# Later queries of batch 1 and later Wo loads at the start of a gated attention and expert kernel

## Chip, cores and metric

One Trainium2 chip, one of its cores, one launch. The metric is the device time of the whole kernel in microseconds (us). Of the core's engines, PE (TensorE) multiplies and transposes, DVE (VectorE), ACT (ScalarE) and POOL (GpSimd) work element by element, and SP (SyncE) issues nearly all DMAs.

## What is computed

```python
def _attend(q, k, v):                      # 32 heads of 16, 8 key heads, T = 256
    scores = einsum('bhqd,bhkd->bhqk', q, k) / sqrt(D) + alibi bias
    scores = where(mask, scores, -inf)     # causal, window 64, two sources side by side
    return einsum('bhqk,bhkd->bhqd', softmax(scores), v)

q = heads(concat([ssm_states, hidden_states]) @ Wq, 32)
k, v = heads(hidden_states @ Wk, 8), heads(hidden_states @ Wv, 8)
ssm_k, ssm_v = heads(ssm_states @ Wsk, 8), heads(ssm_states @ Wsv, 8)
x = x + tanh(g_xattn) * (_attend(q, [ssm_k, k], [ssm_v, v]) @ Wo)      # of layernorm(x), ctx_2048
x = x + tanh(g_ffn) * ffn(layernorm(x))    # router over 128 experts, top 4, 8 shared bases, shared part
```

There are 8 batches of 256 tokens of width 512, in float32.

## The kernel before

Every matrix product is made in three passes over operands split into a high and a low part (`PASSES`), so that a projection of 512 or 1024 rows is a run of 12 or 24 matmuls of 128x256. Each engine has a stream of its own, written out by hand, and the streams meet at semaphores alone.

The attention runs in **slots**: slot n makes the scores of one unit of 64 queries and four heads (`scores(n)`, PE L1917, two matmuls), and DVE takes their maxima (`maxima(n)`, L1448). A batch is 32 slots, a head group g is four. Scores of slot n wait until the maxima of slot n-2 are done, since there are two banks. `scores_turned` (L1944) follows 18 slots later, ACT makes the exponentials (L1099), and `times_v` (L1958) multiplies by the values for two groups at a time. In the gaps of each slot PE makes the projections of the next batch: tables (`EARLY_Q`, `Q_PROJ`, `K_PROJ`, `V_PROJ`) say in which slots. Queries come in four parts r = 0 to 3 of 24 matmuls each. Ahead of slot 0 stand the projections of batch 0, the keys of batch 1, and all 24 matmuls of its first query part (`queries(1, 0, ...)`); the second part lies in slots 0 to 7, three matmuls in each (`PIECES`), the third in slots 9 to 11 and the fourth in 12 to 14. ACT and DVE take each part out of PSUM (`q_high` L1080, `q_low` L1425).

The scores read **stacked** operands, `KS` (k_stack) and `QS` (q_stack), whose rows DATA to FINE hold the three passes of 16 dimensions. They are filled for each head group by DMAs from SP. For the keys it goes through DRAM: `keep_k(b)` (L580) writes three copies of 256 KB, and `stack_k(b, g)` (L596) reads 192 KB back. For the queries there are two ways. In batches 2 to 6 `keep_q(b)` (L586) writes three copies of 512 KB, and `stack_q` (L619) reads 192 KB back for each group. In batches 0, 1 and 7 (`straight(b)`) each group is copied directly within SBUF by three DMAs of 64 KB (`stack_q_direct`, L603). Before slot 0, SP issues in this order: the loads of weights and rows, `keep_k(0)`, the four loads of Wo (L562), for g = 0 to 7 the keys and queries of batch 0, and `keep_k(1)`. In the slots it then issues the stacks of batch 1, group g, in slot 22 + 4g; each waits until PE has done with the same group of batch 0.

The queries of batch 1 have a buffer of their own (`Q1`, second_qT), since those of batch 0 are still being copied. `oT` takes the transposed outputs (`o_high` on ACT, L1110; `o_low` on POOL, L822), first in slot 32. Wo is staged in four pieces in `wo_stage`; ACT and POOL split it in slots 12 to 15 (`SPLIT_WO`), and it is first used in slot 56.

## Time and profile before

| | |
|---|---|
| median of 3 runs | 889.38 us (888.36 to 889.59) |
| the profiled execution | 888.36 us, its span 886.3 us |
| PE busy | 870.2 us, 98% of the span |
| DVE, POOL, ACT busy | 61%, 58%, 45% |
| PE waited for others in the first 75 us | 5.4 us in 14 places |
| first scores, slot 0 | at 34.85 us |
| DMA traffic | 110.17 MB, mean 124 GB/s |

Times in a trace are counted from the start of the span. A matmul's row shows its start and how long it took; since matmuls are pipelined, the distance between two starts, not the duration, is what one costs. What stands in square brackets is how long the engine sat idle before it and what released it. Two states of the PE clock occur, 2.4 GHz (shown as 1.00) and 1.2 GHz (0.50).

### The profile page before, as it was taken

The page shows a single profiled execution, that of the slowest core. Times are in us where ns is not written, and L with a number is a line of the kernel's source. Part 1 is how long each engine was busy: PE and PEld are TensorE (multiplying, and loading weights), DVE is VectorE, ACT ScalarE, POOL GpSimd, SP SyncE. Part 2 cuts the span into 40 slices and gives each one's busy share as a digit, 9 for nine tenths or more (in the row PEclk, how much of TensorE's full clock was granted, in tenths as well). Part 3 has the DMA queues.
Part 4 walks back from the last instruction along what each step waited for, and adds up shares of the span by engine and source line. Part 5 has one row for each costly group of instructions (what it writes and reads, how often), then busy time and mean ns, then how long its engine had stood idle before and what let it go on. Part 6 is the DMA issues. An engine that isn't in the chain of part 4 may idle for free.

```text
span 886.3 us, 17380 instructions
## 1 busy us (share of the span) xinstructions
PE 870.2 (98%) x6662; PEld 757.5 (85%) x6662; DVE 537.9 (61%) x983; ACT 400.5 (45%) x810; POOL 510.1 (58%) x526
## 2 busy tenths in 40 slices
PE   8999999999999999999999999999999999999998
PEld 7889999999999997778888867888888888888886
DVE  6675666666667666533246748466565565565567
ACT  5655555454545455463134243444444444444431
POOL 3861434435353513161679984456788888788741
PEclk9999999999999999899999999999999999999999
DMA  8677576767767655760101244402202021121046
GB/s 269 171 153 183 148 202 185 193 184 188 203 176 203 164 145 131 206 215 13 36 25 48 84 142 158 166 25 71 72 25 96 25 71 35 61 72 48 1 139 241
DMA packets 77947, 110.17 MB, mean 124 GB/s; under 512 B 7329, under 2 KB 49058, under 8 KB 76834
## 3 DMA queue, kind: packets, MB, share of 16 engines
q1 hardware_dynamic: 75656, 108.04, 42.8%
q10 hardware_dynamic: 2210, 1.03, 0.5%
q8 instruction: 53, 0.87, 0.4%
q14 instruction: 28, 0.23, 0.1%
HBM read 71.76 MB, written 32.05 MB: 117 GB/s over the span
## 4 chain that ended last, share of the span: by engine, by line
PE 91%; DVE 4%; issue 1%; POOL 1%; DMA 1%; ACT 1%; SPq 0%; DVEq 0%; POOLq 0%
PE ps_scores L2158 20%; PE ps_proj L1807 13%; PE ps_scoresT L2158 10%; PE ps_scoresT L1944 6%; PE ps_scores L1796 6%; PE ps_o L1958 6%; PE ps_proj L1796 5%; PE ps_scores L1917 5%; PE ps_scoresT L1796 5%; PE ps_proj L2158 5%; PE ps_proj L1865 5%; DMA xn_rows<-in_x 1%; PE ps_o_max L1976 1%; DVE neg_max L1448 1%; PE ps_o_max L1845 1%
## 5 line engine op out<-in xcount | busy, mean ns | idle before, releaser
L1099 ACT ACTIVATE probsT<-ps_scoresT 128x512 f32<-128x512 f32 (+1 forms) x256 | 138.0, 544 | 153.1 <-PE ps_scoresT L1944 148.8
L1448 DVE TENSOR_REDUCE neg_max<-ps_scores 128x2 f32<-128x384 f32 (+1 forms) x256 | 131.2, 516 | 111.1 <-PE ps_scores L1917 110.4
L1315 ACT ACTIVATE part_sums<-ps_scores 128x512 f32<-128x512 f32 x96 | 57.4, 598 | 134.6 <-PE ps_scores L2158 130.2
L1944 PE MATMUL ps_scoresT<-q_stack,k_stack 116*128 116x256 f32 x448 | 106.5, 310 | 1.7 <-ACT probsT L1099 1.6
L1917 PE MATMUL ps_scores<-k_stack,q_stack 114*128 114x192 f32 (+1 forms) x512 | 96.2, 270 | 4.7 <-DVE neg_max L1448 3.8
L816 POOL TENSOR_TENSOR o_normal<-o_blocks,inv_sums 128x256 f32<-128x256 f32 x32 | 19.9, 622 | 130.6 <-DVE inv_sums L1469 130.6
L1917 PEld LDWEIGHTS ps_scores<-k_stack,q_stack 114*128 114x128 f32 x512 | 82.3, 191 | 11.6 <-DVE neg_max L1448 3.8
L962 POOL TENSOR_TENSOR w_expert_lo<-w_sums,w_expert_hi 128x256 fp32r<-128x256 f32 x64 | 63.8, 1007 | 45.5 <-ACT w_expert_hi L1238 45.5
L974 POOL TENSOR_TENSOR big<-big,basis 128x512 f32<-128x512 f32 x56 | 77.5, 1402 | 14.9 <-DVE basis L1746 14.9
L1944 PEld LDWEIGHTS ps_scoresT<-q_stack,k_stack 116*128 116x128 f32 x448 | 70.2, 191 | 6.3 <-ACT probsT L1099 2.8
L1737 DVE TENSOR_TENSOR basis<-part_sums,silu_gate 128x512 f32<-128x512 f32 x32 | 24.2, 755 | 67.3 <-ACT silu_gate L1323 67.3
L1807 PE MATMUL ps_proj<-actT_hi,wq_hi 128*128 128x256 f32 x224 | 63.6, 284 | 0.4 <-DVE second_qT_lo L1425 0.4
L1807 PE MATMUL ps_proj<-actT_lo,wq_hi 128*128 128x256 f32 x224 | 63.3, 283 | 0.0
L1807 PE MATMUL ps_proj<-actT_hi,wq_lo 128*128 128x256 f32 x224 | 63.3, 283 | 0.0
L822 POOL TENSOR_TENSOR oT_lo<-oT_raw,oT_hi 128x256 fp32r<-128x256 f32 x32 | 23.6, 737 | 67.3 <-ACT oT_hi L1110 67.3
L1746 DVE TENSOR_TENSOR basis<-basis,big 128x512 f32<-128x512 f32 x56 | 56.8, 1015 | 1.0
L1958 PE MATMUL ps_o<-probsT,v_ones 128*32 128x128 f32 (+1 forms) x2048 | 56.9, 264 | 0.0
L1958 PEld LDWEIGHTS ps_o<-probsT,v_ones 128*32 128x32 f32 x2048 | 51.5, 111 | 3.6 <-issue 0.3
L1716 DVE TENSOR_TENSOR part_sums<-part_sums,ps_scoresT 128x512 f32<-128x512 f32 x32 | 22.0, 687 | 53.6 <-ACT part_sums L1315 53.6
L962 POOL TENSOR_TENSOR w_expert_lo<-w_raw,w_expert_hi 128x256 fp32r<-128x256 f32 x48 | 45.8, 968 | 11.2 <-ACT w_expert_hi L1238 11.1
L2158 PE MATMUL ps_scores<-xnT_hi,w_expert_lo 128*128 128x512 f32 x128 | 49.8, 389 | 0.0
L2158 PE MATMUL ps_scores<-xnT_hi,w_expert_hi 128*128 128x512 f32 x128 | 49.8, 389 | 0.0
(302 smaller groups left out, 2491.8 us busy)
## 6 DMA issues: line engine op xcount, KB each, us to landing
k_stack<-k_kept SPq DMA_DIRECT2D x64, 192.0 KB, 4.3
big<-coeff_rows SPq DMA_DIRECT2D x8, 1024.0 KB, 4.7
q_stack<-q_kept SPq DMA_DIRECT2D x40, 192.0 KB, 4.2
q_kept<-qT_hi SPq DMA_DIRECT2D x10, 512.0 KB
x_rows<-in_x SPq DMA_DIRECT2D x9, 512.0 KB, 6.5
k_kept<-kT_hi SPq DMA_DIRECT2D x16, 256.0 KB
x_kept<-x_rows SPq DMA_DIRECT2D x16, 256.0 KB, 3.0
w_raw<-in_L_ffn_w_gate SPq DMA_DIRECT2D x16, 256.0 KB, 2.9
```

Of the source, the lines that this page charges most:

```text
L962: pool.tensor_tensor(WS[n % 2]["lo"][:, w, :], w_source(n, w), WS[n % 2]["hi"][:, w, :].bitcast(F32), ALU.subtract).then_inc(e_lo, 1)
L974: pool.tensor_tensor(dst, dst, BS[:, j, :], ALU.add).then_inc(acc_done, 1)
L1099: act.activation(PT[:, g % 2, 2 * j:2 * j + blocks].rearrange("p h f r w -> p (h f r w)"), ST[:, n % 2, 0:blocks].rearrange("p h n -> p (h ...
L1315: act.activation(TP[:, u % 2, j, :], src[:, u % 2, :], ACT.Copy).then_inc(taken, 1)
L1448: dve.tensor_reduce(NM[:, g // 2 % 2, g % 2, 2 * i:2 * i + 2], SA[:, n % 2, :, 0:keys], AX.X, ALU.max, negate=True).then_inc(max_done, 1)
L1746: dve.tensor_tensor(dst, BS[:, j, :], cB[:, k % 2, group_columns(t)], ALU.mult).then_inc(basis_done, 1)
L1796: ins = pe.matmul(out, stat(s, c), mov(m, c), start=c == cs[0] and j == 0, stop=c == cs[-1] and j == PARTS - 1)
L1807: ins = pe.matmul(out, stat(s, c), mov(m, c), start=i == 0, stop=i == len(steps) - 1, skip_group_check=True)
L1917: ins = pe.matmul(SA[:, n % 2, f, 0:2 * (near.stop - near.start)], QS[0:TOP, g, i, f].rearrange("p r w -> p (r w)"), keys[:, near, :].rear ...
L1944: ins = pe.matmul(ST[:, n % 2, v, :], KS[0:ROWS, g, j + v, 1 - v].rearrange("p w s -> p (w s)"), QS[0:ROWS, g, j + v].rearrange("p f r w - ...
L1958: ins = pe.matmul(POB[32 * r:32 * r + 2 * D, n % 2, j * W:j * W + cols_j], VA[:, j, n % HK, :], PT[:, n % 2, 2 * j:2 * j + cols_j // W, :, ...
L2158: ins = pe.matmul(bank[:, u % 2, :], WS[n % 2][s][:, w, c * P:(c + 1) * P], operand(MEETS[w], m, c, g), start=first and c == 0 and j == 0, ...
```

## The change

It does five things.

1. **Queries of batch 1.** Only the first 12 matmuls of part 0 stay ahead of slot 0. The other 12 go into slots 1, 3, 5 and 7, three in each (`EARLY_PIECES`). Parts 1, 2 and 3 lie in slots 9 to 11, 11 to 13 and 13 to 15.
2. **Wo.** Its four loads leave the head of SP's queue. Two are issued in slot 24 and two in slot 28 (`LOAD_WO`), into X1 and a smaller `wo_stage`; they are split in slots 34 to 37 (`SPLIT_WO`). The load of X1's rows in slot 42 waits for the split of the second.
3. **Stacks of batch 1.** Groups 0 and 1 alone are still copied directly (`DIRECT`). For groups 2 to 7 `keep_q(1)` is issued behind `keep_k(1)`, ahead of the slots, and each group is then one read of 192 KB.
4. **Buffers.** `Q1` moves to where `oT` lies. So ACT's first `o_high`, in slot 32, no longer waits for the split of Wo but for `keep_q(1)` to have landed and for the direct copies of groups 0 and 1; POOL's first `x1_normalise` loses its wait for the copies.
5. **Tables.** Rows and context of batches 3 and on are loaded three slots earlier (`LOAD_ROWS`), the gates six slots earlier, tanh four.

```diff
-LOAD_ROWS, STATS = -61, (-51, -50)
+LOAD_ROWS, STATS = -64, (-51, -50)
-EARLY_Q = ((-1, -1, 7), (-1, -1, 8), (9, 10, 11), (12, 13, 14))
-PIECES = 8
+EARLY_Q = ((-1, -1, 7), (9, 10, 11), (11, 12, 13), (13, 14, 15))
+DIRECT = 2
+EARLY_PIECES = {1: 4, 3: 5, 5: 6, 7: 7}
-SPLIT_WO = 12
+LOAD_WO, SPLIT_WO = (24, 28), 34
-TANH, LOAD_GATES = 54, 44
+TANH, LOAD_GATES = 50, 38
...
-    wo_stage = at("wo_stage", 184 * KIB, [P, HC, HID])
+    wo_stage = at("wo_stage", 216 * KIB, [P, 2, HID])
-    Q1 = {h: at(f"second_qT_{h}", (216 - n * 8) * KIB, [P, NB, 2, G, HQ], F32R) for n, h in enumerate(("hi", "lo"))}
+    Q1 = {h: at(f"second_qT_{h}", (184 + n * 4) * KIB, [P, NB, 2, G, HQ], F32R) for n, h in enumerate(("hi", "lo"))}
...
-    def straight(b):
-        return b in (1, B - 1)
+    def straight(b, g):
+        return b == B - 1 or (b == 1 and g < DIRECT)
...
-            sp.wait_ge(q_kept, 16 * PARTS * (b - 1))
+            sp.wait_ge(q_kept, 16 * PARTS * b)
...
-        for n in range(FIRST_O, len(halves)):
-            weight(n)
         for g in range(HK):
             stack_k(0, g)
             stack_q_first(g)
...
         keep_k(1)
+        keep_q(1)
...
+            if n in LOAD_WO:
+                for m in range(2):
+                    weight(FIRST_O + 2 * LOAD_WO.index(n) + m)
...
             elif c == 0:
-                wait_split(act, len(halves) - 1)
+                act.wait_ge(q_kept, 16 * PARTS)
+                for g in range(DIRECT):
+                    act.wait_ge(q_in[g], q_loads(1, g))
...
         keys_values("k", 1, 1)
-        queries(1, 0, 1, 2)
...
-            if n < PIECES:
-                queries(1, 1, n, PIECES)
+            if n in EARLY_PIECES:
+                queries(1, 0, EARLY_PIECES[n], 8)
```

The order of SP's instructions behind the last stack of batch 0, first before and then after the change. k_kept and q_kept are the copies in DRAM.

```order
50 L580 DMA k_kept<-kT_hi 8x16x512 x2
51 L580 DMA k_kept<-kT_lo 8x16x512
52 L596 DMA k_stack<-k_kept 48x4x256
53 L603 DMA q_stack<-second_qT_hi 16x1024
54 L603 DMA q_stack<-second_qT_lo 16x1024
55 L603 DMA q_stack<-second_qT_hi 16x1024
56 L596 DMA k_stack<-k_kept 48x4x256
```

```order
49 L583 DMA k_kept<-kT_hi 8x16x512 x2
50 L583 DMA k_kept<-kT_lo 8x16x512
51 L589 DMA q_kept<-second_qT_hi 8x16x1024
52 L589 DMA q_kept<-second_qT_lo 8x16x1024
53 L589 DMA q_kept<-second_qT_hi 8x16x1024
54 L599 DMA k_stack<-k_kept 48x4x256
55 L606 DMA q_stack<-second_qT_hi 16x1024
56 L606 DMA q_stack<-second_qT_lo 16x1024
57 L606 DMA q_stack<-second_qT_hi 16x1024
58 L565 DMA x_rows<-in_L_xattn_Wo 128x512 x2
59 L599 DMA k_stack<-k_kept 48x4x256
```

Three writes of 512 KB now stand ahead of group 0 of batch 1, and two loads of Wo between its groups 0 and 1. On PE, slots 1 and 2 before the change, and slots 0 to 3 after it:

```order
206 L1917 MATMUL ps_scores<-k_stack,q_stack 128x192 x2
207 L1807 MATMUL ps_proj<-actT_hi,wq_hi 128x256
208 L1807 MATMUL ps_proj<-actT_hi,wq_lo 128x256
209 L1807 MATMUL ps_proj<-actT_lo,wq_hi 128x256
210 L1917 MATMUL ps_scores<-k_stack,q_stack 128x192 x2
211 L1807 MATMUL ps_proj<-actT_hi,wq_hi 128x256
```

```order
191 L1921 MATMUL ps_scores<-k_stack,q_stack 128x128 [waits stack_in0]
192 L1921 MATMUL ps_scores<-k_stack,q_stack 128x128
193 L1921 MATMUL ps_scores<-k_stack,q_stack 128x192 x2
194 L1811 MATMUL ps_proj<-actT_hi,wq_hi 128x256
195 L1811 MATMUL ps_proj<-actT_hi,wq_lo 128x256
196 L1811 MATMUL ps_proj<-actT_lo,wq_hi 128x256
197 L1921 MATMUL ps_scores<-k_stack,q_stack 128x192 [waits max_done]
198 L1921 MATMUL ps_scores<-k_stack,q_stack 128x192
199 L1921 MATMUL ps_scores<-k_stack,q_stack 128x192 [waits max_done]
200 L1921 MATMUL ps_scores<-k_stack,q_stack 128x192
```

Before, three matmuls of a projection stand behind each pair of scores; after, behind every second pair.

## Rows read from the trace of the kernel before

**Rows 1.** Page, parts 1 (busy us, share) and 5 (busy us, mean ns, idle before).
```profile
PE 870.2 (98%) x6662; PEld 757.5 (85%) x6662; DVE 537.9 (61%) x983; ACT 400.5 (45%) x810; POOL 510.1 (58%) x526
...
L1448 DVE TENSOR_REDUCE neg_max<-ps_scores 128x2 f32<-128x384 f32 (+1 forms) x256 | 131.2, 516 | 111.1 <-PE ps_scores L1917 110.4
```

**Rows 2.** Waits of PE, whole span: engine, line, waited for, us in total, times, longest.
```profile
PE ps_scores L1917 <- DVE neg_max L1448: 3.8, 10, 1.1
```

**Rows 3.** Timeline of PE, slots 0 to 17: start, us taken, engine, line, operation.
```profile
34.03 0.28 PE L1807 MATMUL ps_proj<-actT_hi,wq_lo 128*128 128x256 f32 x1
34.15 0.28 PE L1807 MATMUL ps_proj<-actT_lo,wq_hi 128*128 128x256 f32 x1
34.85 0.44 PE L1917 MATMUL ps_scores<-k_stack,q_stack 114*128 114x128 f32 x2 [0.41 <-DMA q_stack<-qT_hi]
...
37.88 0.44 PE L1917 MATMUL ps_scores<-k_stack,q_stack 114*128 114x128 f32 x2 [0.44 <-DMA q_stack<-qT_hi]
...
41.84 0.39 PE L1807 MATMUL ps_proj<-actT_hi,wq_hi 128*128 128x256 f32 x1 [0.38 <-DVE second_qT_lo L1425]
...
49.82 0.47 PE L1917 MATMUL ps_scores<-k_stack,q_stack 114*128 114x192 f32 x2 [0.46 <-DVE neg_max L1448]
```

**Rows 4.** Timeline of DVE around slot 0.
```profile
27.50 0.78 DVE L1425 TENSOR_TENSOR qT_lo<-ps_scoresT,qT_hi 128x256 fp32r<-128x256 f32 x2
...
33.71 0.69 DVE L1418 TENSOR_TENSOR kT_lo<-ps_proj,kT_hi 128x512 fp32r<-128x512 f32 x1 [2.47 <-ACT kT_hi L1071]
35.32 0.42 DVE L1448 TENSOR_REDUCE neg_max<-ps_scores 128x2 f32<-128x256 f32 x1 [0.92 <-PE ps_scores L1917]
```

**Rows 5.** Timeline of SP's DMA issues: start, us that the issue took.
```profile
20.91 1.37 SPq L580 DMA_DIRECT2D k_kept<-kT_hi  x2
...
29.68 0.65 SPq L596 DMA_DIRECT2D k_stack<-k_kept  x1
30.43 0.62 SPq L603 DMA_DIRECT2D q_stack<-qT_hi  x1
...
52.14 1.33 SPq L580 DMA_DIRECT2D k_kept<-kT_hi  x2
...
60.03 0.60 SPq L596 DMA_DIRECT2D k_stack<-k_kept  x1
```

**Rows 6.** Timeline of SP, batch 2: its query writes and the stacks behind them.
```profile
93.37 0.65 SPq L586 DMA_DIRECT2D q_kept<-qT_hi  x1
...
97.65 1.71 SPq L596 DMA_DIRECT2D k_stack<-k_kept  x1
106.34 0.35 SPq L619 DMA_DIRECT2D q_stack<-q_kept  x1
```

**Rows 7.** The k_stack load issued at 97.65: from issue to landing, us.
```profile
DMA to landing us min/median/max: 11.0/11.0/11.0
```

**Rows 8.** Windows: stretch, us, busy of each engine, granted clock, DMA share, GB/s.
```profile
55.00:58.00 3.00, 3.00 (x28) 2.95 (x26) 1.76 (x4) 2.46 (x5) 2.97 (x3) 1.00 0.52 188
101.00:104.00 3.00, 3.00 (x60) 2.69 (x62) 1.71 (x4) 0.67 (x3) 0.00 (x0) 1.00 0.53 203
350.00:352.00 2.00, 1.05 (x8) 0.84 (x8) 1.11 (x4) 0.97 (x3) 2.00 (x3) 1.00 0.84 269
...
354.00:356.00 2.00, 2.00 (x33) 1.74 (x35) 1.16 (x2) 0.61 (x2) 0.00 (x0) 0.50 0.95 255
```

**Rows 9.** Timeline of PE: slot 32, a times_v at 2.4 GHz, one at 1.2 GHz.
```profile
66.50 0.34 PE L1917 MATMUL ps_scores<-k_stack,q_stack 114*128 114x128 f32 x2
...
69.59 1.74 PE L1958 MATMUL ps_o<-probsT,v_ones 128*32 128x128 f32 x64
...
354.61 2.73 PE L1958 MATMUL ps_o<-probsT,v_ones 128*32 128x128 f32 x64
```

**Rows 10.** Timeline of ACT in slots 32 and 33.
```profile
67.66 0.41 ACT L1110 ACTIVATE oT_hi<-oT_raw 128x256 fp32r<-128x256 f32 x1
68.55 0.39 ACT L1099 ACTIVATE probsT<-ps_scoresT 128x256 f32<-128x256 f32 x1 [0.48 <-PE ps_scoresT L1944]
```

More of the change, by code:

```diff
@@ L175, in projections @@
 def projections():
-    order = [("k", 0, 0), ("v", 0, 0)] + [("q", 0, r) for r in range(G)] + [("k", 1, 0), ("q", 1, 0), ("q", 1, 1)]
+    order = [("k", 0, 0), ("v", 0, 0)] + [("q", 0, r) for r in range(G)] + [("k", 1, 0), ("q", 1, 0)]
     for n in range(SLOTS):
@@ L382, in staging @@
         if n >= FIRST_O:
-            return wo_stage[:, n - FIRST_O, :]
+            return (X1, wo_stage)[(n - FIRST_O) // 2][:, (n - FIRST_O) % 2, :]
         return stage[:, n % 8, :]
@@ L438, in queries_of, with q_loads @@
         return Q1 if b == 1 else Q
-    def straight(b):
-        return b in (1, B - 1)
-    def q_loads(b):
-        return 16 * sum(PARTS if straight(i) else 1 for i in range(1, b + 1))
+    def straight(b, g):
+        return b == B - 1 or (b == 1 and g < DIRECT)
+    def q_loads(b, g):
+        return 16 * sum(PARTS if straight(i, g) else 1 for i in range(1, b + 1))
     def wait_rows(eng, g):
@@ L557, in weight @@
                 wait_split(sp, n - 8)
+            if n == FIRST_O:
+                sp.wait_ge(prep_t, 2 * TB)
             src = halves[n][0]
@@ L613, in stack_q @@
             sp.wait_ge(st_mm, (b - 1) * UNITS + NB * (g + 1))
-            if straight(b):
+            if straight(b, g):
                 sp.wait_ge(pj_done, passed("q", b, G - 1))
@@ L675, in _ @@
                 else:
-                    sp.wait_ge(prep_t, 2 * TB)
+                    wait_split(sp, FIRST_O + 1)
                 sp.dma_start(X1[:], x_t[:, b]).then_inc(x1_in, 16)
@@ L692, in _ @@
                 for g in range(HK):
-                    sp.wait_ge(q_in[g], q_loads(B - 1))
+                    sp.wait_ge(q_in[g], q_loads(B - 1, g))
                 router = cols(a["L0_ffn_w_router"], 0)
@@ L834, in x1_normalise @@
                 pool.wait_ge(xT_mm, TB * b)
-            elif t == 0:
-                for g in range(HK):
-                    pool.wait_ge(q_in[g], q_loads(1))
             if 1 <= b <= SPILLED:
@@ L1077, in q_high @@
             elif b >= 3 and r == 0:
-                act.wait_ge(q_kept, 16 * PARTS * (b - 2))
+                act.wait_ge(q_kept, 16 * PARTS * (b - 1))
             act.wait_ge(q_mm, G * b + r + 1)
@@ L1910, in scores @@
                 if b >= 1:
-                    pe.wait_ge(q_in[g], q_loads(b))
+                    pe.wait_ge(q_in[g], q_loads(b, g))
             if n >= 2:
@@ L2069, in _ @@
                     b = queries_due(n, r, part)
-                    if b is not None and (b > 1 or r > 1):
+                    if b is not None and (b, r) != (1, 0):
                         queries(b, r, part)
```

## Prediction

> **What bounds the kernel now.** The page comes first: PE is busy for 98% of the span [rows 1], and the change neither adds nor removes a matmul. So it can only take away or add time in which PE stands still, or time at its lower clock. The waits of PE over the whole span say where it stands [rows 2]: the longest sum, for the maxima, is 3.8 us in ten places. Third, the timeline of PE in slots 0 to 17 shows the waits that this change can reach [rows 3]: 0.41 and 0.44 us for the query copies of groups 0 and 1, 0.38 us for a bank, 0.46 us for a maximum. Each costs more than its idle time: from the start at 34.15 to that at 34.85 are 0.70 us where a matmul costs 0.12. Counted so, they are worth some 3 us, the ceiling of the gain at the front. Then I read the queue of SP, since the change loads it in a new place.
>
> **The front, slots 0 to 17.** One matmul of a projection costs 0.12 us (34.03 to 34.15 [rows 3]). Twelve of them leave the stretch ahead of slot 0, so PE reaches slot 0 at 34.27 - 12 x 0.12 = 32.8 us. Is the first stack there? Its keys were issued at 29.68 us, when the writes of `keep_k(0)` had landed, 8.8 us after their first issue at 20.91 [rows 5]. Wo's 1 MB was loaded beside them. 768 KB at the 188 GB/s of such writes alone [rows 8] take 4.1 us, so without Wo they should be there at about 27.5. The query copies then wait for the low part of the queries, at 27.50 + 0.78 = 28.3 us [rows 4], and go out at 28.4 instead of 30.43 [rows 5]: 2.1 us earlier, and with them all stacks of batch 0, each group four issues behind the last. The first copies, which PE got at 34.85, it now gets at 32.8. That fits.
>
> But DVE is not ready. It takes the low part of batch 1's keys at 33.71, whose matmuls end when they did, and is free at 34.3 instead of starting its first maximum at 35.32 [rows 4]. The gain there is 1.0 us. From then on slots 0 to 7 hold 16 score matmuls and 12 others, about 3.1 us of PE, but eight maxima in a ring with the scores, at 0.516 us each [rows 1]: slot 8 comes at about 38 us, PE stands still for about 2 us on the way, and slots 9 to 15 then hold 72 projection matmuls, 8.6 us, instead of 48. The bank wait of 0.38 us and the wait at 49.82 [rows 3] go, because matmuls now stand where the scores were alone. Carried through, slot 18 starts about 0.8 us earlier. Bounds: 1.9 us earlier, if half of PE's still time in slots 0 to 7 is filled better than I assume; 0.5 us later, if group 2 is late by a slow issue. I take **-0.8 us**.
>
> **The stacks of batch 1.** SP ends with batch 0's stacks at 50.0 instead of 52.1 and issues `keep_k(1)`. Behind it now stand three writes of 512 KB, and in front of slot 32 still the keys and direct copies of group 0. What such a queue does is to be seen in batch 2 [rows 6]: first query write issued at 93.37, all landed at 106.34, 13.0 us later; the key load issued behind them, at 97.65, landed 11.0 us after its issue [rows 7], that is after the writes, not beside them. While queries or keys are written the DMA share is 0.53 and 0.52 and the rate 203 and 188 GB/s [rows 8]: half of the 16 engines work, and a load that needs all 16 waits for that half. For batch 1: keys' writes end 2 us earlier than before, at 57.5 (before 60.03 at the latest [rows 5]); 1.5 MB at 203 GB/s are 7.7 us; the writes end at 65.2. Then come group 0's keys and its three copies, about 2.1 us with their landing. Group 0 is there at 67.3. PE wants it in slot 32, at 66.50 [rows 9] less 0.8, or 65.7. **+1.6 us**. Bounds: 0, if the key writes finish by 54.5 and the queries' follow at once; 3.5, if the query writes also show the 13.0 us of batch 2, counted from the release of the keys' half.
>
> On this the Trainium skill has two rules, both in "DMA: Bandwidth & Descriptors". In "Why a DMA increments its semaphore by 16 and not by 1" a DMA runs on the largest number of engines up to 16 that divides its slowest dimension: these writes are 8x16x1024 (the order shows it), so on 8, and the trace agrees with its share of 0.53. Its "Specifications" give about 27 GiB/s for an engine. As an estimate from that page 8 engines move 232 GB/s, the writes take 6.8 us, and the wait would be 0.7 us instead of 1.6; the trace's 203 GB/s stands against it, and the sum goes by the trace.
>
> **ACT's new wait.** In slot 32 ACT makes the first `o_high`, before at 67.66 [rows 10]. It now waits for the copies of group 1 too, and these stand behind two loads of Wo (512 KB) and group 1's keys: some 3 us behind group 0, at about 70.4. ACT gets to it at 67.3 + 1.2 = 68.5. Queued behind it is the exponential of slot 33, before at 68.55 for 0.39 us, which `times_v` at 69.59 [rows 9, 10] waits for: the slack is 0.65 us. Now `o_high` ends at 70.8 and the exponential at 71.2, while PE could use it at 70.5. **+0.7 us**. Bounds: 0 (the slack covers it, or group 0 is late by so much that group 1 is not later still) and 2.5 us (issues of 1.7 us each, as the one at 97.65 [rows 6], for the four ahead of it).
>
> **The clock.** In the 2 us from 350 the PE was busy for 1.05, and from 354 to 356 the granted clock was 0.50, that is 1.2 instead of 2.4 GHz [rows 8]; a `times_v` then took 2.73 instead of 1.74 us [rows 9]. A stand of 1.6 us in slot 32, with sparse slots (29 to 31) before it and a second wait soon after, is a gap of the same size. I take one such fall, with one slow `times_v`, **+1.0 us**. Bounds: 0, and 1.7 if the whole low stretch is filled with matmuls.
>
> **Edits at nothing.** The split of Wo leaves ACT and POOL in slots 12 to 15, where nobody waited for them, and comes to slots 34 to 37; POOL's `scale_outputs` is about 2 us later there, and DVE's turn of it in slot 37 half a us, one slot ahead of the next scores that could feel it. If that cover is gone it costs 0.5 us. Rows and context three slots earlier, gates and tanh: their users are ten and more slots behind them. Five issues fewer on SP are only worth something where SP is late, which is behind slot 32.
>
> **Sum:** -0.8 + 1.6 + 0.7 + 1.0 = +2.5 us. Against the profiled execution that is 888.36 + 2.5 = 890.9 us; this was the fastest of the three, 1.0 us under the median, so I give it against the median: 889.38 + 2.5 = **891.9 us**.
>
> **Rivals.**
> 1. *The stacks are in time.* If the writes of keys and queries end by 63, group 0 lands before 65.7 and only the front is left: -0.8, 888.6 us. For it: batch 2's slow start may belong to its writes alone, and keys ahead of them may cover it; SP is 2 us earlier. Against it: 11.0 us [rows 7]. It decides when the writes end before 63.5. With the front at its best, -1.9 to -2.5 us, it would be 887.2 us.
> 2. *The waits come, the clock stays.* +1.5 us, 890.9 us. For it: other sparse stretches of the front do not lower the clock.
> 3. *Issues behind a full queue are slow.* The load at 97.65 took 1.71 us to issue [rows 6], the others 0.6. With such issues for all of groups 0 and 1, group 1 lands some 3 us later and ACT's wait counts in full: +2.5 + 3.0 = +5.5 us, 894.9 us.
> 4. *Slots 0 to 7 are too sparse*, and the clock falls there too: +1.0 to +1.7 on any of the others.
>
> **How the numbers follow.** The forecast has 0.36, the first rival 0.24 at 888.6 and 0.10 at 887.2, the second 0.18, the third and fourth together 0.12. What a measurement of this kernel can tell from no change is about 0.2%, 1.8 us: below 887.6 is faster, above 891.2 slower. Slower: the forecast, the third and fourth, and the upper end of the second, 0.53. Faster: the best front and a little of the first, 0.13. The rest, 0.34, within. Range: from 887.6 (1.8 us gained, near the best front) to 895.2 (the third rival and a little more).
>
> **What the profile would show.** Right: PE's first scores at 32.8 and first maximum at 34.3; slot 8 at 38; slot 18 under a us earlier; PE idle for one to three us ahead of slot 32 with a DMA as its releaser; `o_high` idle for a us or more behind q_stack copies; a granted clock of 0.50 somewhere from 66 to 75. Wrong: group 0 of batch 1 landed before PE asked (first rival); DVE not the pace of slots 0 to 7; a stand at another place, such as slots 34 to 38, which would be the split of Wo.

## The result and the profile after

The changed kernel takes 894.24 us (median of 6 runs, 892.6 to 894.64), the kernel before, run beside it, 889.25 us (885.26 to 890.02). The ratio is 1.006, with a 95% interval of 1.0042 to 1.0079: **slower by 0.6%**. The profiled execution took 892.44 us, its span is 890.4 us.

The page of the changed kernel, parts 1 and 5, against [rows 1]:

```profile
PE 872.0 (98%) x6662; PEld 758.9 (85%) x6662; DVE 539.8 (61%) x983; ACT 400.1 (45%) x810; POOL 509.9 (57%) x526
...
L1452 DVE TENSOR_REDUCE neg_max<-ps_scores 128x2 f32<-128x384 f32 (+1 forms) x256 | 130.9, 516 | 110.2 <-PE ps_scores L1921 109.5
```

The instructions are the same in number and PE's share is the same. PE is busy 1.8 us longer with the same work, so part of the loss is a low clock and not idle time. The waits of PE in the first 75 us (engine, line, waited for: us in total, times, longest) name the rest:

```profile
PE ps_o L1962 <- ACT probsT L1101: 1.3, 1, 1.3
PE ps_scores L1921 <- DVE neg_max L1452: 1.2, 3, 0.7
PE ps_scores L1921 <- DMA q_stack<-qT_hi: 1.2, 1, 1.2
...
PE ps_scores L1921 <- issue: 0.7, 1, 0.7
...
PE ps_proj L1869 <- DMA q_stack<-second_qT_hi: 0.2, 1, 0.2
```

To place the loss, I read the same instructions in both timelines of PE: the first scores of slots 0, 20, 28 and 32, and the start of the fourth `times_v`.

| PE starts, us | slot 0 | slot 20 | slot 28 | slot 32 | fourth `times_v` |
|---|---|---|---|---|---|
| before | 34.85 | 52.17 | 61.86 | 66.50 | 91.85 |
| after | 32.40 | 53.67 | 63.34 | 68.79 | 95.76 |
| difference | -2.45 | +1.50 | +1.48 | +2.29 | +3.91 |

Behind that the two run in step: from the fourth `times_v` to the end of the span are 794.4 us before and 794.6 us after. So there are three losses: 3.9 us between slots 0 and 20 (1.4 of it are the 12 matmuls that moved there), 0.8 us in slot 32, and 1.6 us right behind it.

**The front.** Timeline of PE in the changed kernel, slots 0 to 8 (columns as in [rows 3]):

```profile
32.40 0.69 PE L1921 MATMUL ps_scores<-k_stack,q_stack 114*128 114x128 f32 x4
...
34.13 0.93 PE L1921 MATMUL ps_scores<-k_stack,q_stack 114*128 114x192 f32 x4 [0.66 <-DVE neg_max L1452]
...
36.65 0.69 PE L1921 MATMUL ps_scores<-k_stack,q_stack 114*128 114x128 f32 x4 [1.21 <-DMA q_stack<-qT_hi]
...
38.63 0.28 PE L1811 MATMUL ps_proj<-actT_lo,wq_hi 128*128 128x256 f32 x1
38.81 1.14 PE L1921 MATMUL ps_scores<-k_stack,q_stack 114*128 114x128 f32 x4
...
41.24 0.41 PE L1811 MATMUL ps_proj<-actT_hi,wq_hi 128*128 128x256 f32 x1
41.45 0.41 PE L1811 MATMUL ps_proj<-actT_hi,wq_lo 128*128 128x256 f32 x1
```

Windows of the same kernel (columns as in [rows 8]):

```profile
35.00:38.80 3.80, 2.59 (x18) 2.05 (x18) 2.24 (x6) 3.78 (x8) 3.80 (x5) 1.00 0.65 129
38.80:42.20 3.40, 3.40 (x17) 3.35 (x17) 1.96 (x6) 1.32 (x4) 1.11 (x2) 0.50 0.71 141
42.20:45.00 2.80, 2.80 (x25) 2.80 (x25) 1.90 (x4) 0.00 (x0) 0.00 (x0) 0.99 0.85 260
```

PE stood for 0.66 us behind DVE and for 1.21 us behind the query copies of group 1, and was busy for 2.59 of 3.80 us. The copy it stood for is group 1's last. SP issued it in time, but it was long on its way (SP's row, and the landing times of group 1's last two copies, of which the 4.5 us are this one's):

```profile
32.09 0.58 SPq L606 DMA_DIRECT2D q_stack<-qT_hi  x1
...
DMA to landing us min/median/max: 2.9/3.7/4.5
```

Then the granted clock was 0.50, 1.2 GHz, from 38.8 to 42.2 us. In that stretch the distance between two matmuls of a projection is 0.21 us (41.24 to 41.45) instead of 0.12. Low for 3.4 us costs 1.7 us.

**Slot 32 and `o_high`.** SP's issues in the changed kernel (start, us taken):

```profile
52.25 0.75 SPq L589 DMA_DIRECT2D q_kept<-second_qT_hi  x1
...
58.03 0.59 SPq L599 DMA_DIRECT2D k_stack<-k_kept  x1
59.13 0.66 SPq L606 DMA_DIRECT2D q_stack<-second_qT_hi  x1
59.84 1.35 SPq L606 DMA_DIRECT2D q_stack<-second_qT_lo  x1
61.23 2.21 SPq L606 DMA_DIRECT2D q_stack<-second_qT_hi  x1
63.55 1.24 SPq L565 DMA_DIRECT2D x_rows<-in_L_xattn_Wo  x2
```

The key load of 58.03, from issue to landing in us:

```profile
DMA to landing us min/median/max: 9.9/9.9/9.9
```

A window of the same kernel while the writes run, with a DMA share of 0.55:

```profile
54.00:57.00 3.00, 3.00 (x27) 3.00 (x27) 1.72 (x4) 1.72 (x4) 0.71 (x1) 1.00 0.55 207
```

The timeline of PE, slot 32 and the second half of the `times_v` behind it:

```profile
68.79 0.41 PE L1921 MATMUL ps_scores<-k_stack,q_stack 114*128 114x128 f32 x2 [0.66 <-issue]
...
74.26 0.97 PE L1962 MATMUL ps_o<-probsT,v_ones 128*32 128x128 f32 x32 [1.33 <-ACT probsT L1101]
```

And that of ACT, `o_high` and the exponential behind it:

```profile
73.52 0.42 ACT L1114 ACTIVATE oT_hi<-oT_raw 128x256 fp32r<-128x256 f32 x1 [3.40 <-DMA q_stack<-second_qT_hi]
73.84 0.37 ACT L1101 ACTIVATE probsT<-ps_scoresT 128x256 f32<-128x256 f32 x1
```

Group 0's keys land at 58.03 + 9.9 = 67.9 us and its last copy at 68.7; PE starts at 68.79. ACT stands still for 3.40 us for the copies of group 1, and the exponential behind `o_high` holds up the second half of `times_v` by 1.33 us.

### The profile page after: what moved, and what is told of

It reads as the page before. It is cut to its first block, busy times and chain, and to the rows that moved or that the text cites. A ratio compares the mean times of both kernels' runs of the same rounds, so it can differ in the third digit from the quotient of the medians.

```text
span 890.4 us, 17369 instructions
## 1 busy us (share of the span) xinstructions
PE 872.0 (98%) x6662; PEld 758.9 (85%) x6662; DVE 539.8 (61%) x983; ACT 400.1 (45%) x810; POOL 509.9 (57%) x526
## 4 chain that ended last, share of the span: by engine, by line
PE 89%; DVE 3%; DMA 3%; issue 1%; SPq 1%; POOL 1%; ACT 1%; DVEq 0%; POOLq 0%; ACTq 0%
PE ps_scores L2161 20%; PE ps_proj L1811 13%; PE ps_scoresT L2161 10%; PE ps_scoresT L1948 6%; PE ps_scores L1800 6%; PE ps_o L1962 6%; PE ps_proj L1800 5%; PE ps_scores L1921 5%; PE ps_scoresT L1800 5%; PE ps_proj L2161 5%; PE ps_proj L1869 4%; DMA xn_rows<-in_x 1%; DMA q_stack<-second_qT_hi 1%; DVE neg_max L1452 1%; PE ps_o_max L1980 1%
## 5 line engine op out<-in xcount | busy, mean ns | idle before, releaser
L821 POOL TENSOR_TENSOR o_normal<-o_blocks,inv_sums 128x256 f32<-128x256 f32 x32 | 19.9, 621 | 129.7 <-DVE inv_sums L1473 129.7
L1741 DVE TENSOR_TENSOR basis<-part_sums,silu_gate 128x512 f32<-128x512 f32 x32 | 24.2, 755 | 67.3 <-ACT silu_gate L1327 67.3
L1811 PE MATMUL ps_proj<-actT_lo,wq_hi 128*128 128x256 f32 x224 | 63.7, 284 | 0.0
L1962 PE MATMUL ps_o<-probsT,v_ones 128*32 128x128 f32 (+1 forms) x2048 | 57.5, 265 | 1.3 <-ACT probsT L1101 1.3
L1750 DVE TENSOR_TENSOR basis<-basis,big 128x512 f32<-128x512 f32 x56 | 56.8, 1015 | 1.0
```

Source lines behind the costliest of these rows:

```text
L1750: dve.tensor_tensor(dst, BS[:, j, :], cB[:, k % 2, group_columns(t)], ALU.mult).then_inc(basis_done, 1)
L1811: ins = pe.matmul(out, stat(s, c), mov(m, c), start=i == 0, stop=i == len(steps) - 1, skip_group_check=True)
L1962: ins = pe.matmul(POB[32 * r:32 * r + 2 * D, n % 2, j * W:j * W + cols_j], VA[:, j, n % HK, :], PT[:, n % 2, 2 * j:2 * j + cols_j // W, :, ...
```

## The experiments

One table first, all from profiled executions. "Low" is the stretch before 90 us in which the granted clock was 0.50. The last columns are the medians and the ratio to the kernel before, run beside each; medians of different rows come from different sets of runs, so kernels are compared by the ratio. e1 to e5 and e11 have 4 to 6 runs each, the others 12.

| run | slot 0 | slot 20 | slot 32 | fourth `times_v` | low | median | ratio (95%) |
|---|---|---|---|---|---|---|---|
| before | 34.85 | 52.17 | 66.50 | 91.85 | none | | |
| after | 32.40 | 53.67 | 68.79 | 95.76 | 38.8 to 42.2 | 894.24 | 1.0060 (1.0042, 1.0079) |
| e1 | 33.41 | 50.53 | 69.81 | 96.70 | 66.2 to 73.0 | 892.09 | 1.0063 (1.0038, 1.0089) |
| e2 | 34.32 | 56.13 | 70.46 | 95.79 | 35.1 to 45.3 | 892.13 | 1.0062 (1.0039, 1.0085) |
| e3 | 33.14 | 55.29 | 69.62 | 95.88 | none | 891.83 | 1.0060 (1.0035, 1.0085) |
| e4 | 33.80 | 52.94 | 72.57 | 100.84 | 68.7 to 78.9 | 895.38 | 1.0093 (1.0064, 1.0122) |
| e5 | 32.84 | 51.57 | 69.15 | 97.12 | 68.0 to 74.8 | 894.15 | 1.0069 (1.0046, 1.0091) |
| e6 | 32.28 | 52.19 | 66.52 | 91.85 | 36.5 to 39.9 | 887.61 | 0.9987 (0.9971, 1.0004) |
| e7 | 34.04 | 51.18 | 65.49 | 90.82 | none | 887.52 | 0.9982 (0.9968, 0.9995) |
| e8 | 34.37 | 51.91 | 66.25 | 93.14 | none | 887.06 | 0.9991 (0.9976, 1.0007) |
| e9 | 33.87 | 50.99 | 65.29 | 94.27 | 74.7 to 78.1 | 887.37 | 0.9982 (0.9969, 0.9995) |
| e10 | 33.35 | 50.47 | 67.13 | 93.47 | 66.0 to 69.4 | 890.64 | 1.0020 (1.0009, 1.0032) |
| e11 | 33.58 | 52.54 | 66.85 | 104.39 | 76.1 to 86.3 | 897.86 | 1.0105 (1.0085, 1.0125) |
| e12 | 34.44 | 51.56 | 65.87 | 91.20 | none | 886.57 | 0.9979 (0.9964, 0.9994) |

### e1 and e2: each half of the change at the front

e1 is the changed kernel with the query tables of before:

```diff
-EARLY_Q = ((-1, -1, 7), (9, 10, 11), (11, 12, 13), (13, 14, 15))
-EARLY_PIECES = {1: 4, 3: 5, 5: 6, 7: 7}
+EARLY_Q = ((-1, -1, 7), (-1, -1, 8), (9, 10, 11), (12, 13, 14))
+PIECES = 8
```

> The changed kernel with the query tables of before: all 24 matmuls of part 0 of batch 1 ahead of slot 0, part 1 in slots 0 to 7 with three matmuls in each, parts 2 and 3 in slots 9 to 14. Wo late, query writes and new buffers stay. Theory A (the front is too sparse): slot 0 now starts at 34.3 us, slots 0 to 8 run at 0.58 us each, the granted clock stays at 1.00 from 30 to 50 us, slot 18 starts at about 50.0 instead of 51.95 us, and the time falls by 1 to 2 us, if the waits at slots 32 to 34 don't take it back. Rival B (the queue of DMAs alone made the loss, slots 0 to 18 are only shifted work): slot 18 stays near 51.9 us and the time as it is. Rival C (the stacks of batch 1 come at a fixed time): slot 18 is earlier, but PE then waits longer ahead of slot 32 and the exponential of slot 33, so that slot 36 starts when it does in the changed kernel and the time is the same within 0.5 us.

The front is 3.1 us faster than in the changed kernel (slot 20 at 50.53 against 53.67), with no low clock there. But slot 32 starts 1.0 us **later**, and the ratio is the same 1.006. The waits of PE in e1 (columns as above):

```profile
PE ps_scores L1921 <- issue: 4.8, 1, 4.8
```

Two windows of e1, before and in this stand:

```profile
62.00:66.00 4.00, 2.56 (x15) 1.79 (x14) 2.64 (x7) 1.32 (x3) 2.46 (x2) 1.00 0.70 200
66.00:70.00 4.00, 0.18 (x1) 0.22 (x2) 0.00 (x0) 0.00 (x0) 0.00 (x0) 0.52 1.02 233
```

PE comes to slot 32 early, stands for 4.8 us until 69.81 (the profile names no releaser), and the clock falls there, as the prediction had it for this place. Group 0's last copy, issued from 62.92 to 64.81, is what lands last, at 69.7. What the front gains, slot 32 takes.

e2 is the kernel before with the new query tables alone (the opposite of the diff above).

> The kernel before with only the new query tables (12 matmuls of part 0 in slots 1, 3, 5 and 7, parts 1 to 3 in slots 9 to 15); Wo early, all copies of batch 1 direct. Theory A (sparse front): slots 0 to 7 are paced by the maxima and by the stacks, which come as in the kernel before (slot 8 at 40.5 us); slots 9 to 15 carry 24 matmuls more, 2.9 us, so slot 18 starts 1 to 2.5 us later than 50.78, more if the clock falls, and the time is 1 to 3 us above the kernel before. Rival B (front harmless): slot 18 within 0.5 us of 50.78 and the same time.

From slot 0 to slot 20 it takes 21.8 us; before it was 17.3. Of the 4.5 us more the 12 moved matmuls are 1.4. The other 3.1 lie in a stretch with 10.2 us of low clock (half of that, 5.1 us, is the most that it can cost) and 0.49 us of standing in slot 4. A window of e2 just as the low clock begins:

```profile
32.00:35.00 3.00, 1.43 (x13) 1.23 (x12) 0.89 (x2) 2.90 (x6) 3.00 (x5) 1.00 0.64 141
35.00:38.00 3.00, 2.51 (x13) 2.16 (x11) 1.71 (x4) 3.00 (x8) 3.00 (x4) 0.52 0.79 158
```

PE was busy for 1.43 of 3 us and then ran at 1.2 GHz. The timeline of PE in e2, slot 0:

```profile
34.32 0.69 PE L1917 MATMUL ps_scores<-k_stack,q_stack 114*128 114x128 f32 x4 [1.57 <-DMA q_stack<-qT_hi]
```

The new query places alone cost 0.6%, without any query write in the queue: its slot 32 has no wait, and from there to the fourth `times_v` it takes 25.33 us, as the kernel before (25.35). Theory A held against its rival, with a loss of 5.5 us by the ratio where it had 1 to 3. So the late group 0 is not the only way to lose 0.6%. In e2 Wo is still loaded early, group 0 of batch 0 lands only at 34.2 us, and PE, which has 12 matmuls fewer ahead of slot 0, stands there for 1.57 us.

### e3: filling the sparse slots

The changed kernel with three idle matmuls of 128x256 each in slots 0, 2, 4 and 6, whose result nobody reads:

```diff
+            if n in (0, 2, 4, 6):
+                ones = VA[:, 0].rearrange("p g e -> p (g e)")
+                for _ in range(3):
+                    pe.matmul(POB[:, :, :].rearrange("p h n -> p (h n)")[:, 0:T], ones[:, 0:P], ones[:, 0:T], start=True, stop=True)
```

> The changed kernel with three idle matmuls of 128x256 (ones by ones, into a free bank) added in each of slots 0, 2, 4 and 6, where PE stands still for the maxima; 1.4 us of work that nobody reads. Theory A1 (the fall of the clock is what costs at the front): the granted clock stays at 1.00 between 38 and 43 us, slot 12 starts 1 to 1.7 us earlier than 45.27 us, slot 18 at about 50.6. Rival A2 (only the pace of the maxima and the late copies of group 1 cost): the clock stays up but slot 12 starts no earlier, or later by the 1.4 us added. If slot 18 is earlier by 1.5 us, the time falls by 0 to 1.5 us, by how much the stacks of batch 1 let it.

The clock stays high up to 350 us. This one trace doesn't show that the filling did it, since e4, e5 and e11 have the unfilled front of the changed kernel and no fall there either. The mean granted clock of all runs says more: 0.996 to 1.000 in the five runs of e3, 0.992 or 0.994 in the eight of the changed kernel on record. But the time didn't follow. The 12 idle matmuls, 1.4 us, and whatever else is longer take more than the fall did: 22.2 us from slot 0 to slot 20 against 21.3. Rival A2 won. PE then comes to slot 32 at 69.62, when group 0's last copy has landed at 69.5, so nearly without a stand. The fourth `times_v` is where it was (95.88 against 95.76), and so is the ratio.

### e4: Wo out of the way of group 1

```diff
-LOAD_WO, SPLIT_WO = (24, 28), 34
+LOAD_WO, SPLIT_WO = (26, 30), 34
```

> The changed kernel with the loads of Wo issued in slots 26 and 30 instead of 24 and 28, that is behind the stacks of group 1 and group 2 and no longer ahead of them. Theory (ACT's wait for the copies of group 1 is made by what stands ahead of them on SP): the copies of group 1 are issued 1.3 us earlier, o_high starts 1.2 to 2 us earlier than 73.52 us, PE's wait of 1.33 us at times_v of slot 34 goes, the time falls by about 1.3 us. Rival (the copies of group 1 wait for the query writes like those of group 0): o_high at 73 us or later, no change in the time.

Neither the theory nor its rival foresaw the result, 1.0093; its interval overlaps that of the changed kernel, so that it is slower than that isn't shown. `o_high` (at 74.29, not 1.2 to 2 us earlier than 73.52) no longer stands idle, but only because PE is later: group 0 is. Its query writes were issued 1.0 us later (53.25 against 52.25) and took longer, and the last of the direct copies landed at 72.5 instead of 68.7. The timeline of PE in e4, slot 32:

```profile
72.57 0.66 PE L1921 MATMUL ps_scores<-k_stack,q_stack 114*128 114x128 f32 x2 [5.16 <-DMA k_stack<-k_kept]
```

The window in which this stand ends, at 1.2 GHz:

```profile
70.00:74.00 4.00, 1.43 (x7) 1.46 (x8) 0.42 (x1) 0.20 (x1) 0.00 (x0) 0.50 0.99 215
```

That the moved Wo made the writes slower isn't shown: it is issued after group 0. The executions with the same writes differ (below), and 4 runs are few. What is shown is that this order of the loads behind the writes doesn't help.

### e5: only group 0 copied directly

```diff
-DIRECT = 2
+DIRECT = 1
```

> The changed kernel with group 0 of batch 1 alone copied directly; group 1 is one read of q_kept. ACT's first o_high then waits for the q_kept writes and for group 0. Theory (a group's landing is set by the query writes, which landed at 66.9 us, and the wait of o_high for group 1, 3.40 us idle and 1.33 us of it on PE, is a cost of its own): group 0 lands at 68.7 as before, o_high starts by about 70.5 instead of 73.5, the wait of PE for probsT at 74.3 goes, and the whole is 1.3 us shorter, about 892.9. Rival (the time lost at o_high is only the time lost at slot 32 seen a second time): the same as the changed kernel, 894.2.

The part on `o_high` held: it starts without a wait and 2.7 us earlier, and PE's wait for probsT is gone. The timeline of PE in e5, slot 32:

```profile
69.15 0.66 PE L1921 MATMUL ps_scores<-k_stack,q_stack 114*128 114x128 f32 x2 [3.10 <-DMA k_stack<-k_kept]
```

The timeline of ACT in e5, `o_high`:

```profile
70.87 0.41 ACT L1114 ACTIVATE oT_hi<-oT_raw 128x256 fp32r<-128x256 f32 x1
```

The forecast of 1.3 us gained fell: 894.15 us, ratio 1.0069. In this execution the front had no low clock (slot 20 at 51.57), PE came early, stood for 3.10 us, and the clock was low from 68.0 to 74.8 instead. From slot 32 to the fourth `times_v` are 27.97 us, more than the 26.97 of the changed kernel, although the wait on ACT is gone. The median is that of the rival, the trace has the mechanism of the theory. My reading is that the wait is a cost of its own, and that what is saved went to the stand and the fall at slot 32. One trace doesn't prove it; the mean granted clock of its runs, 0.988 to 0.992 against 0.992 and 0.994 in the changed kernel, fits it.

### e6 and e7: writes of 128 rows

In both kernels the three passes of a dimension are laid side by side in DRAM, and in the rows DATA to FINE. A write of keys is then 128 rows of 512 and one of queries 128 rows of 1024, not 8 blocks of 16 rows. Bytes and number of DMAs are the same. e6 is the changed kernel so, e7 the kernel before:

```diff
-    q_kept_d = nc.dram_tensor("q_kept", (2, HK, PARTS, D, 2 * NB * 2 * W), F32).ap()
+    q_kept_d = nc.dram_tensor("q_kept", (2, HK, D, PARTS, 2 * NB * 2 * W), F32).ap()
...
-                sp.dma_start(q_kept_d[b % 2, :, j], queries_of(b)[part][:].rearrange("p i f r w -> p (i f r w)").bitcast(F32)
+                sp.dma_start(q_kept_d[b % 2, :, :, j].rearrange("g d n -> (g d) n"), queries_of(b)[part][:].rearrange("p i f r w -> p (i f r w)").bitcast(F32)
...
-                sp.dma_start(QS[DATA + j * D:DATA + (j + 1) * D, g].rearrange("p i f r w -> p (i f r w)").bitcast(F32),
+                sp.dma_start(QS[DATA + j:FINE:PARTS, g].rearrange("p i f r w -> p (i f r w)").bitcast(F32),
```

> The changed kernel with the layout in DRAM and of the rows DATA to FINE changed from (pass, dimension) to (dimension, pass), so that a write of keys or queries is 128 rows of 512 or 1024 instead of 8 blocks of 16. Theory (the writes run on half of the engines and this sets group 0's landing): the DMA share in the stretch of the query writes rises from 0.55 to over 0.8, they land at about 63 instead of 66.9, group 0 at about 65 instead of 68.7, before PE asks for it in slot 32; issues of 0.6 us instead of 1.3 and 2.2; group 1 lands about 3 us earlier, so o_high costs PE little. 2.2 us gained, about 892. The clock fall at 39 us stays. Rival (the rate of 200 GB/s is that of DRAM or of the queue, not of the number of engines): landing at 67 as before, 894.2.

This is the run that bears most on the main cause. Two windows of e6, while the keys and the queries are written (the second holds group 0's load and copies too):

```profile
50.00:54.00 4.00, 3.80 (x29) 3.34 (x29) 3.26 (x8) 2.12 (x5) 3.24 (x2) 1.00 1.03 326
54.00:58.00 4.00, 4.00 (x36) 3.98 (x35) 2.29 (x5) 3.05 (x6) 0.00 (x0) 1.00 1.01 371
```

SP's issues for group 0 in e6:

```profile
54.31 0.57 SPq L599 DMA_DIRECT2D k_stack<-k_kept  x1
55.38 0.88 SPq L606 DMA_DIRECT2D q_stack<-second_qT_hi  x1
56.31 0.58 SPq L606 DMA_DIRECT2D q_stack<-second_qT_lo  x1
56.93 0.59 SPq L606 DMA_DIRECT2D q_stack<-second_qT_hi  x1
```

The timeline of ACT in e6, `o_high`, with no idle time before it:

```profile
67.68 0.41 ACT L1114 ACTIVATE oT_hi<-oT_raw 128x256 fp32r<-128x256 f32 x1
```

The share nearly doubles, from 0.55 to 1.01, and the rate rises from 207 to 371 GB/s. On this the Trainium skill's rule in "DMA: Bandwidth & Descriptors", section "Why a DMA increments its semaphore by 16 and not by 1", holds: 128 is a multiple of 16, so all 16 engines should work, and the share of 1.01 agrees.

Group 0's copies, 3.6 us at most from issue to landing, are there at 60.4 instead of 68.7, eight us earlier, where I had expected 65. PE doesn't wait in slot 32, `o_high` starts at 67.68 as in [rows 10], and the fourth `times_v` at 91.85, as before the change. The low clock in front is still there (36.5 to 39.9). The new layout gave back all of the 3.9 us that the profile had lost. But only 2.4 of them are the waits of slot 32 (0.8) and behind it (1.6). The other 1.5 were there at slot 20 already (52.19 against 53.67), before the query writes had landed: PE has no wait for query copies in front. The layout also changes the key writes of batch 0 (group 0's keys are issued at 24.07 us instead of 27.46) and the rows that the direct copies fill, and e6 doesn't tell these apart from the luck of one execution: e5, with narrow writes, came to slot 20 earlier still, at 51.57.

The gain is more than the 2.2 us expected: 6.6 us between the medians 894.24 and 887.61, which come from two sets of runs. The mean granted clock rose with it, from 0.992 or 0.994 to between 0.994 and 1.000 in the 12 runs of e6.

e6 and e2 have the same query places. In e6 Wo is late and group 0 of batch 0 in time, and slot 0 starts at 32.28 instead of 34.32. That may be why the new places cost 0.6% in one kernel and nothing that shows in the other; no run separates it.

> The kernel before with the same layout as the run above. Theory: the first key writes (issued at 20.9, last landing about 29.6) end up to 3 us earlier, so that the first group is in its place when PE has ended its projections at 34.3, and DVE with its first maximum at 34.3 to 35 is the next thing late: 0.4 to 0.9 us gained, 888.4 against 889.2. Rival (a load beside them, Wo, takes what they leave, and SP's issues pace the stacks): no change, 889.2. If the ratio is over 1.0, the wide writes cost elsewhere (batches 2 to 6).

e7 is faster than the kernel before by 0.2%, with an interval below 1: the wide writes need no other part of the change. Slot 0 starts at 34.04, `times_v` at 90.82, 1.0 us earlier. No kernel below with parts of the change added to it is faster than e7's 0.9982 by more than the noise.

### e8: the late Wo alone

```diff
-SPLIT_WO = 12
+SPLIT_WO = 28
...
-        for n in range(FIRST_O, len(halves)):
-            weight(n)
         for g in range(HK):
...
         keep_k(1)
+        for n in range(FIRST_O, len(halves)):
+            weight(n)
```

> The kernel before with one part of the change only: the four loads of Wo issued behind keep_k(1) instead of ahead of the first stack, and split in slots 28 to 31. All queries as before, all stacks of batch 1 copied directly, no query writes. Theory (the gain of the moved Wo at the front is real, as in the run with the old queries, where slot 28 started at 59.6 instead of 61.24, and only the query writes lost it again): slot 28 at 59.6, group 0 lands by 64.5 and slot 32 starts at 65 instead of 66.5: 1.6 us faster than before, 887.6 against 889.2, ratio 0.998. Rival (Wo behind the keys delays the stacks of batch 1 as the query writes do): slot 32 waits 1 to 3 us for q_stack, ratio 1.000 or above, and perhaps a fall of the clock.

Slot 32 starts at 66.25, 0.25 us earlier and not 1.5; and the wait came that ACT had not shown before, this time behind POOL. The timeline of ACT in e8:

```profile
70.91 0.42 ACT L1110 ACTIVATE oT_hi<-oT_raw 128x256 fp32r<-128x256 f32 x1 [3.40 <-POOL wo_lo L847]
```

The timeline of POOL in e8, Wo's low parts:

```profile
65.81 5.01 POOL L847 TENSOR_TENSOR wo_lo<-wo_stage,wo_hi 128x512 fp32r<-128x512 f32 x4
```

The gain at the front is smaller than I took from e1. Kernels with the same order of instructions ahead of slot 0 reach it at different times: e1 and e8 at 33.41 and 34.37, and with wide writes e9 and e12 at 33.87 and 34.44. e1 was an early one. The profile would make e8 slower by 1.3 us, the ratio is 0.9991 and doesn't tell it from 1. The profiled execution, 889.41 us, is the third slowest of its 12, whose median is 887.06, so the profile may overstate the loss.

### e9, e10 and e12: looking for a faster kernel

e9 is the changed kernel with the diffs of e1 and of e6 together: old queries, wide writes.

> The changed kernel with the wide writes (rows of keys and queries laid out by dimension, then pass) and with the queries of batch 1 where the kernel before had them. Theory (two separate losses: the clock fall at 36 to 42 us from the new query places, and the late group 0 from the narrow writes; both are gone here): no fall of the clock ahead of 350 us, slot 28 at 59.6 as in the run with the old queries, group 0 landed by 61, o_high not idle for a DMA. The times_v that starts at 91.85 in the kernel before starts at 90.2, and at 91.85 with wide writes and the new queries: 1.6 us faster than before, ratio 0.998. Rival (the new query places cost nothing once the stacks are in time, since DVE paces slots 0 to 7 in both): the same as with wide writes alone.

The ratio is 0.9982, as the theory had it. No clock fall in front, slot 32 at 65.29 without a wait, as expected. But in the profiled execution, 890.92 us and the slowest of its 12, PE stood still in the middle of a projection, with nothing that the profile shows it to wait for, and the clock fell at 74.7. The timeline of PE in e9:

```profile
70.86 0.28 PE L1811 MATMUL ps_proj<-actT_hi,wq_hi 128*128 128x256 f32 x1
73.00 0.39 PE L1811 MATMUL ps_proj<-actT_hi,wq_lo 128*128 128x256 f32 x1 [1.85 <-issue]
```

The window of e9 around the stop:

```profile
70.00:74.00 4.00, 2.15 (x27) 1.88 (x16) 1.43 (x3) 2.23 (x4) 2.02 (x2) 1.00 1.06 264
```

e12 is e9 with the tables of the change's fifth part back:

```diff
-LOAD_ROWS, STATS = -64, (-51, -50)
+LOAD_ROWS, STATS = -61, (-51, -50)
-TANH, LOAD_GATES = 50, 38
+TANH, LOAD_GATES = 54, 44
```

> The run with the old queries and the wide writes, and the tables of the fifth part of the change back at their old numbers (rows and context -61, gates 44, tanh 54). In that run PE stood still for 1.9 us in the middle of a projection, at 70.9 to 73.0, with nothing to wait for, while the DMA share was 1.01 to 1.06 from 66 to 74 us (0.61 to 0.63 in the kernel before), and the clock fell at 74.7. Theory (the loads of rows and context, three slots earlier, keep the DMA engines full there, and PE's own instructions come late through them): without them at 64.4 the share falls under 0.9 by 70 us, the stop and the fall go, the times_v that starts at 91.85 in the kernel before (at 94.27 in that run) starts at 90.3 to 90.6, and the total is 1 us or more below that run, ratio to before 0.9970. Rival (a stop of one execution that the median doesn't hold): the stop is gone too, but the ratio is the 0.998 of that run; or the times_v is at 91.2 because the rows now collide with the reads of groups 3 to 5.

The share from 66 to 70 us is 0.53 now, against 1.01 in e9, and the stop is gone. A full share alone doesn't bring it: it is 1.04 in e12 from 74 to 78 us and 1.05 in e6 from 66 to 70, without a stop. But the ratio is 0.9979 against 0.9982 for e9, the same within the intervals: the rival is right, a stop of one execution that the median doesn't hold. The fifth part of the change costs nothing that can be measured here, with the old queries and wide writes, as the prediction had it. The forecast of 0.9970 fell. The fourth `times_v` came at 91.20 and not at 90.3 to 90.6, since this execution reached slot 0 only at 34.44; from there on it takes 56.8 us, as e7 does (90.82 - 34.04), against 57.0 before.

e10 is e8 with the wide writes of e7 and with Wo split in slots 26 to 29:

```diff
-SPLIT_WO = 28
+SPLIT_WO = 26
```

> The kernel before with the wide writes and with Wo issued behind keep_k(1) and split in slots 26 to 29. All stacks of batch 1 copied directly, no query writes. Theory: with Wo split two slots earlier than in the run with the late Wo alone, POOL (5.0 us for four low parts, there 65.8 to 70.8) ends by about 66, so o_high at 66.2 isn't held up and the 1.33 us of PE at times_v go. The times_v at 91.85 starts at 90.2 to 90.8: 1.0 to 1.6 us faster than before, ratio 0.9985. Rival (POOL is then late with the low part of the context instead, and PE waits in slots 29 to 31): no better than the run with the late Wo alone, 93.14.

Its rival won: 1.0020, slower than before. With the split two slots earlier ACT and POOL are late for others. Waits of PE in e10:

```profile
PE ps_scoresT L1944 <- ACT probsT L1099: 1.2, 2, 0.9
PE ps_proj L1865 <- POOL actT_lo L809: 1.1, 1, 1.1
```

The clock fell at 66.0. So of the places for Wo's split that were tried with wide writes, slots 26 to 29 cost 0.4% against slots 12 to 15 (e7) and 34 to 37 (e12), which don't differ.

### e11: the query writes behind groups 0 and 1

```diff
         keep_k(1)
-        keep_q(1)
...
+            if n == UNITS + STACKED[DIRECT - 1]:
+                keep_q(1)
```

> The changed kernel, narrow writes, but with the three query writes issued behind the stacks of groups 0 and 1 (slot 26) instead of ahead of them. Theory (the queue order alone makes group 0 late): group 0 lands by 65 and group 1 by 68, PE doesn't wait in slot 32; the query writes, 9 us of half the engines, land only at about 73 to 75, and o_high waits for them, starting at 74 or later: its wait takes the place of the other, PE idle for 3 to 5 us at times_v, and the clock falls there. The times_v at 91.85 in the kernel before starts at 95 to 97, total 894 to 896: no cure. Rival (o_high's wait is mostly covered, as it was for 2.1 of 3.4 us): 891 to 892.

The first half held: group 0 landed at 63.7, and slot 32 starts at 66.85 without a wait. The second was worse than expected. SP's first write and its read of group 2, which goes out when the writes have landed:

```profile
65.69 0.65 SPq L589 DMA_DIRECT2D q_kept<-second_qT_hi  x1
...
79.41 0.34 SPq L622 DMA_DIRECT2D q_stack<-q_kept  x1
```

The timeline of ACT in e11, `o_high`:

```profile
79.42 0.42 ACT L1115 ACTIVATE oT_hi<-oT_raw 128x256 fp32r<-128x256 f32 x1 [11.30 <-DMA q_kept<-second_qT_hi]
```

The timeline of PE in e11, the second half of `times_v`:

```profile
80.16 1.72 PE L1963 MATMUL ps_o<-probsT,v_ones 128*32 128x128 f32 x32 [9.24 <-ACT probsT L1102]
```

The writes take 13.7 us from issue to landing with other loads beside them, and PE stands for 9.24 us: ratio 1.0105. So with narrow writes ahead of group 0 slot 32 waits, and with them behind it it doesn't: their place in the queue and their slowness cause the wait together. Changing the order alone moves it to `o_high`.

## Why the prediction was right, step by step

The sign was right, and the measured 894.24 us lies in the range of 887.6 to 895.2, 2.3 us above the forecast of 891.9. The two waits that it named are in the trace, though the profile puts the 0.66 us of slot 32 down to "issue" and not to a DMA (group 0's last copy had landed 0.1 us before PE went on). But of its four terms one had the wrong sign and the others another size, and that the total lies so near is in part luck: the wait of slot 32 was taken 0.8 us too high, ACT's 0.9 us too low, and the fall of the clock, priced at slot 32, came in front.

**The front, -0.8 us: wrong.** It is +1.5 us, outside the bounds of -1.9 to +0.5. Slot 0 at 32.40, the first maximum at 33.66 and slot 8 at about 39 are near the 32.8, 34.3 and 38 of the prediction. What failed here is the step from "PE stands still for about 2 us on the way" to the sum: I took the still time as idle time alone. It was followed by 3.4 us at 1.2 GHz, 1.7 us lost. Rival 4 had this mechanism, at +1.0 to +1.7, and I gave it too little weight. The other thing that it hadn't is the wait of 1.21 us for group 1 of batch 0, whose last copy took 4.5 us to land. My upper bound had a slow issue for group 2; there is one, 1.24 us at 34.06, but it comes behind group 1 and PE didn't wait for it. The loss is no fixed cost. From slot 0 to slot 20, kernels with the new queries take 18.7 to 19.1 us where no fall came (e4, e5, e11) and 19.9 to 21.8 where one did (after, e2, e6); before it is 17.3 and 12 matmuls are 1.4. e3, with idle matmuls and no fall, takes 22.2.

**The stacks of batch 1, +1.6 us: mechanism right, size off.** The writes landed at about 67, not 65.2, and group 0 at 68.7, not 67.3. The wait was worth only +0.8 us because PE came 1.5 us late. In e1, where it came early, the stand was 4.8 us. The term that was mis-sized is the rate. The keys' writes landed at 58.0, not 57.5 (the load issued at 58.03 waited for them), and the queries' at 66.9, 8.9 us for three times 512 KB, which is 176 GB/s, not 203. The 203 GB/s were read from a window with writes alone; here group 0's keys and copies were issued beside them. e6 shows that with wide writes the group is in time; that it is the number of engines which counts in the new layout is read from its share of 1.01, and no run tests it apart from the rest of the layout.

**ACT's wait, +0.7 us: mechanism right, but 1.6 us.** `o_high` started at 73.52, not 70.4: group 1's copies were 3.0 us later than I had them. The stand of 3.40 us had 2.1 us of cover; 1.33 us reached PE.

**The clock, +1.0 us: right in kind, in the wrong place.** No fall near slot 32 in the changed kernel, one at 38.8. In the profiled executions it fell either in front (after, e2, e6) or at slot 32, where PE stood for 3.1 to 5.2 us (e1, e4, e5), and in e3 in neither place. In the kernels with narrow query writes ahead of it, group 0 lands at 68.7 to 72.5 us whatever PE does, and in after, e1, e3 and e5 at 68.7 to 69.7. So what PE gains in front it stands longer for in slot 32, and the total hardly depends on which of the two comes. That fits the ratios of 1.006 to 1.007 of these four; it is argued from single traces. The prediction added the front's gain and the wait to its sum once each, but took the clock as a cost of the stand alone.

**Edits at nothing: right.** e12 against e9 for the tables. With Wo's split in slots 34 to 37, e12 (0.9979) doesn't differ from e7 (0.9982), which has it in 12 to 15.

**The rivals.** The first (stacks in time) failed for the kernel as written and is what e6 measures. The third, slow issues behind a full queue, is there in the trace (1.35 and 2.21 us at 59.84 and 61.23), and at 894.9 us its total is closer than the forecast's. The terms as measured are +1.5, +0.8 and +1.6, or +3.9 us. The ratio gives +5.3 (3.7 to 7.0). The profiled execution is the fastest of the changed kernel's, with a mean granted clock of 0.994; five of the eight runs on record have 0.992. As an estimate from these, 0.002 of 890 us are 1.8 us more in those runs, enough for what is over 3.9. Where the clock fell in them isn't known.
